# Layer-norm statistics moved from VectorE to ScalarE, with new slacks, a new opening and a new end, in a kernel of two FFNs around a selective scan

## The reference

```python
x = x + 0.5 * ffn(layernorm(x))
x = x + mamba(layernorm(x))
x = x + 0.5 * ffn(layernorm(x))

def ffn(x):    # 512 -> 1408 -> 512, ternary weights with a scale per row
    return ((silu((x @ gate_w.T) * gate_s) * ((x @ up_w.T) * up_s)) @ down_w.T) * down_s

def mamba(x):  # I = 1024 channels, N = 16 states, R = 128
    h, gate = split(x @ W_in.T)
    u = silu(causal_conv4(h) + conv_b)
    ts, B, C = split(u @ Wx.T);  ts, B, C = rms(ts), rms(B), rms(C)
    delta = softplus(ts @ Wdt.T + dt_bias)
    # per channel i, state n:  s = exp(delta * A[i, n]) * s + delta * u * B[n];  y += s * C[n]
    return ((y + D * u) * silu(gate)) @ Wout.T
```

## Time and profile before

| what | value |
|---|---|
| median of three runs | 3033.19 us |
| profiled execution, its own time | 3031.56 us |
| span from first to last instruction | 3029.6 us |
| busy: PE / DVE / POOL / ACT | 81% / 82% / 75% / 58% of the span |
| mean granted TensorE clock | 0.888 of full speed |
| first scan instruction | 207.15 us |
| x of the last chunk stored to `out` (issue) | 3022.30 us |

### The profile page before, as it was taken

The page is one execution under the profiler, slowest core; times in us unless marked ns, Lnnn a source line. Parts: engine busy times, 40 slices in busy tenths (PEclk is TensorE's granted clock), DMA queues, the critical chain, the costliest instruction groups (busy, mean ns, idle before and its releaser), DMA issues. The chain is left out here.

```text
span 3029.6 us, 37464 instructions
## 1 busy us (share of the span) xinstructions
PE 2454.4 (81%) x12266; PEld 1988.6 (66%) x12266; DVE 2487.0 (82%) x3129; ACT 1769.5 (58%) x3005; POOL 2262.2 (75%) x1372
## 2 busy tenths in 40 slices
PE   7567776967787799778998899888997796697878
PEld 5456555756666677667776677666775675576666
DVE  5539897879988889599977899799987988899952
ACT  5456566565765667465566667665566566654522
POOL 2237767886997778777888679978898778997832
PEclk9778797978798899898998899999998897798899
DMA  7543562664286645884478555974478555556464
GB/s 278 193 160 130 185 221 67 199 228 163 89 277 235 224 138 179 309 275 157 136 255 298 206 167 172 321 280 144 156 245 291 187 165 187 202 181 242 136 219 136
DMA packets 294953, 608.70 MB, mean 201 GB/s; under 512 B 23008, under 2 KB 23776, under 8 KB 294752
## 3 DMA queue, kind: packets, MB, share of 16 engines
q1 hardware_dynamic: 294752, 606.23, 59.6%
HBM read 453.57 MB, written 152.57 MB: 200 GB/s over the span
## 5 line engine op out<-in xcount | busy, mean ns | idle before, releaser
L1104 POOL TENSOR_TENSOR sbuf<-dus,bring 128x1024 f32<-128x1024 f32 x512 | 1219.1, 2395 | 314.6 <-PE pt L1144 229.2
L512 PE MATMUL pm<-xT,wring 128*128 128x512 f32 x4352 | 1132.5, 409 | 89.2 <-DVE xT L535 30.4
L512 PEld LDWEIGHTS pm<-xT,wring 128*128 128x128 f32 x4352 | 821.5, 195 | 262.9 <-issue 83.8
L1118 ACT ACTIVATE pa<-dls,cst 128x512 f32<-128x512 f32 x1024 | 692.0, 688 | 482.5 <-DVE sbuf L1127 439.6
L1144 PE MATMUL pt<-ident,sbuf 128*128 128x128 f32 x4096 | 678.3, 306 | 263.4 <-DVE sbuf L1127 154.2
L1144 PEld LDWEIGHTS pt<-ident,sbuf 128*128 128x128 f32 x4096 | 532.1, 157 | 424.4 <-DVE sbuf L1127 204.5
L1127 DVE TENSOR_TENSOR_SCAN sbuf<-pa,carry,sbuf 128x512 f32<-128x512 f32 x512 | 635.7, 1269 | 72.7 <-POOL sbuf L1104 38.1
L1127 DVE TENSOR_TENSOR_SCAN sbuf<-pa,sbuf 128x512 f32<-128x512 f32 x512 | 605.4, 1209 | 83.0 <-ACT pa L1118 46.8
L584 PE MATMUL pm<-wring,act 128*128 128x512 f32 x2176 | 588.7, 416 | 58.9 <-DVE hd L1040 28.2
L1155 DVE SCALAR_TENSOR_TENSOR acc<-pt,cT,acc 128x512 f32<-128x512 f32 x768 | 549.1, 741 | 95.9 <-PE pt L1144 87.9
L584 PEld LDWEIGHTS pm<-wring,act 128*128 128x128 f32 x2176 | 410.5, 197 | 157.5 <-DVE hd L1040 33.4
(11 more groups left out here) (133 smaller groups left out, 2086.9 us busy)
## 6 DMA issues: line engine op xcount, KB each, us to landing
wring<-wsp SPq DMA_DIRECT2D x408, 512.0 KB, 4.3
bring<-b_d SPq DMA_DIRECT2D x256, 256.0 KB, 3.8
xn_d<-tb SPq DMA_DIRECT2D x24, 1024.0 KB, 9.0
xnb<-xn_d SPq DMA_DIRECT2D x21, 1024.0 KB, 7.4
x_d<-tb SPq DMA_DIRECT2D x16, 1024.0 KB, 5.7
u_d<-hd SPq DMA_DIRECT2D x64, 256.0 KB, 3.8
sg_d<-hd SPq DMA_DIRECT2D x64, 256.0 KB, 4.0
tb<-x_d SPq DMA_DIRECT2D x16, 1024.0 KB, 7.1
```

The source lines that it names most:

```text
L512: f = lambda e, pw=pw, px=px, k=k, first=(i == 1), end=(i == total): e.matmul(pm[b][:, 0:n], lhs(pw, k), rhs(px, k), start=first, stop=end)
L1104: t_p = S.op("pool", lambda e, s2=s2, s3=s3, h=h: e.tensor_tensor(sbuf[:, s3, h * m:(h + 1) * m, :], dus[:, h * m:(h + 1) * m, :], bring[: ...
L1118: t_e = S.op("act", lambda e, k=k, i=i, pb=pb, n=n: e.activation(pa[pb][:, :], dls[:, k, :], ACT.Exp, scale=col(C_A + i * N + n)), dl_tok[ ...
```

## The change

`STATS = "act"`: except for three norms (chunk input 0, chunk 0 after FFN 1, the last chunk after the scan) ScalarE takes the statistics: a pass with a row sum per tile, POOL makes -mean of it, and a second pass squares the differences and sums them. Both passes write their elementwise result to `tb[:, 0:4]`, which must be free for it. The other edits: thread T gets a slack of 0.3 on VectorE and 0.5 on PE; `prep_in` of chunks 1 and 2 too is fed straight from `tb` (DIRECT); chunk 0's convolution works in PSUM with three tiles open and its projection steps behind the loop; parts 0 and 1 of chunk 0's softplus go into thread L, without the 12 us, and their u is loaded into `dus` beforehand; `dus` is freed and loaded by halves; in the last `post` blocks 4 to 7 are made inside the projection, in the banks `pt` and `pa`; in the last `tail` two of four additions go to VectorE and each tile is stored by itself.

```diff
-SLACK_T = 0.0
+SLACK_T = 0.3
+SLACK_S = 0.0
+SLACK_TP = 0.5
+STATS = "act"
+DIRECT = (0, 1, 2)
+DEPTH0 = 3
+SOFT0 = True
+LASTPOST = True
+LASTOUT = True
-WITH_CONV = (0,)
+WITH_CONV = ()
-... "t": dict(pe=0, dve=3, act=3, pool=3, slack_dve=SLACK_T), "s": dict(act=4, dve=4, pool=4)}
+... "t": dict(pe=0, dve=3, act=3, pool=3, slack_dve=SLACK_T, slack_pe=SLACK_TP), "s": dict(act=4, dve=4, pool=4, slack_dve=SLACK_S)}
...
+        def stats(tt, t_x, free, quick=True):
+            if quick:
+                t = L.op("dve", lambda e: e.bn_stats(st[:, tt, :], tb[:, 4 + tt, :]), t_x)
+                return L.op("dve", lambda e: e.bn_aggr(mv[:, tt, :], st[:, tt, :]), t, *free.get("mv", ()), n=16)
+            return L.op("act", lambda e: e.activation(
+                tb[:, tt, :], tb[:, 4 + tt, :], ACT.Copy, accum_out=mv[:, tt, 0:1]), t_x,
+                *free.get("mv", ()), *free.get("tb0", ()), more=0.25)
+        def normalise(free, ln_out, s, c, t_mv, quick=True):
+            m = 1.0 if quick else 1.0 / H
+            t = L.op("pool", lambda e: e.tensor_scalar(nb[:, :], mv[:, :, 0], -m, 0.0, ALU.mult, ALU.add), t_mv, ...
+            if not quick:
+                for tt in range(4):
+                    t_mv = L.op("act", lambda e, tt=tt: e.activation(
+                        tb[:, tt, :], tb[:, 4 + tt, :], ACT.Square, bias=nb[:, tt:tt + 1],
+                        accum_out=mv[:, tt, 1:2]), t, more=0.25)
+            t = L.op("pool", lambda e: e.tensor_scalar(ve[:, :], mv[:, :, 1], m, EPS, ALU.mult, ALU.add), t_mv, n=16)
...
+            quick = STATS == "dve" or c == 0                                  # pre_norm
+                quick = STATS == "dve" or (s, c) in ((1, 0), (2, NCH - 1))    # tail
+                at_end = LASTOUT and last_out and c == NCH - 1
                 for k in range(nk):
+                    if middle and k == 4:
+                        middle()
...
-                        t_r = M.op("pool", lambda e, tt=tt: e.tensor_tensor(
+                        t_r = M.op("dve" if at_end and tt % 2 else "pool", lambda e, tt=tt: e.tensor_tensor(
                             tb[:, 4 + tt, :], tb[:, tt, :], tb[:, 4 + tt, :], ALU.add), t_o, t_x)
+                        if at_end:
+                            t_s = M.dma(st_x, x_dst[c * TC + tt * P:c * TC + (tt + 1) * P, :], tb[:, 4 + tt, :], t_r)
...
-                t_xT = ready_xT((1, c)) if c else make_xT(first_xn[-1], tb)
+                t_xT = make_xT(first_xn[c], tb) if c in DIRECT else ready_xT((1, c))
...
-                    if opened:
-                        finish()
                     opened.append((i, r, b, t_c))
-                    if c not in TWO_OPEN:
+                    while len(opened) >= (1 if c else DEPTH0):
                         finish()
...
+                ahead = SOFT0 and (c, part) in ((0, 0), (0, 1))
+                X = L if ahead else D
+                stay = c == 0 and part < 2
+                if stay:
+                    t_u = D.dma(l_du[i0], dus[:, i0:i0 + 2, :], u_d[c, i0:i0 + 2].rearrange("k p n -> p k n"),
+                                u_tok[i0], u_tok[i0 + 1], t_small[0])
...
-                t_l = D.op("act", lambda e: e.activation(e_, e_, ACT.Ln, bias=1.0), t_q,
-                           n=n, table="ln")
+                t_l = X.op("act", lambda e: e.activation(e_, e_, ACT.Ln, bias=1.0), t_q,
+                           n=n, table="ln0" if ahead else "ln")
...
+                def second_half():            # post, chunk 7: passed to tail as middle
+                    for i in range(4, NI):
+                        block(i)              # turned in pt and pa instead of pm
...
-                                          *sf("du"))
+                                          *sf(("du", k // 2)))
...
+                        if n == N - 1:
+                            sfree["du", h] = (t_p,)
+                            if ig == 0:
+                                for k in range(h * m, (h + 1) * m):
+                                    load_u(1, k)
...
-            INPLACE = ("prep_in", 0), ("ffn2", NCH - 1)
+            INPLACE = *(("prep_in", c) for c in DIRECT), ("ffn2", NCH - 1)
```

More of the change, by code:

```diff
@@ L560, in build, with tail @@
             last_xn = []
-            first_xn = list(begun.get("first_xn", []))
+            first_xn = dict(begun.get("first_xn", {}))
             free.update(begun.get("free", first_free))
-            def tail(nk, first_piece, scale, t_act, x_src, x_dst, s, c, last_out=False):
+            def tail(nk, first_piece, scale, t_act, x_src, x_dst, s, c, last_out=False, middle=None):
                 if first:
@@ L606, in tail @@
                     if not last_out:
-                        t_mv = stats(tt, t_r, free)
+                        t_mv = stats(tt, t_r, free, quick)
+                if at_end:
+                    stores.append(t_s)
+                    return
                 if scale is None:
@@ L616, in tail @@
                 else:
-                    t_xn = normalise(free, ln_out, s, c, t_mv)
-                    if s == 1 and c == 0:
-                        first_xn.append(t_xn)
+                    t_xn = normalise(free, ln_out, s, c, t_mv, quick)
+                    if s == 1 and c in DIRECT:
+                        first_xn[c] = t_xn
                     if s == 2 and c == NCH - 1:
@@ L707, in prep_in @@
                 even = c % 2 == 0
-                t_xT = ready_xT((1, c)) if c else make_xT(first_xn[-1], tb)
+                t_xT = make_xT(first_xn[c], tb) if c in DIRECT else ready_xT((1, c))
                 if c + 1 < NCH:
                     pre_norm(free, ln_out, c + 1)
-                if c == 0 and c not in WITH_CONV:
+                if c in DIRECT and c not in WITH_CONV:
                     prefetch(0)
@@ L820, in prep_in @@
                         x_step(i - XLAG)
-                if opened:
+                while opened:
                     finish()
@@ L988, in softplus_steps @@
                 yield True
-                t_l = D.op("dve" if c == 0 else "pool", lambda e: e.tensor_tensor(e_, e_, w_, ALU.subtract),
+                t_l = X.op("dve" if c == 0 else "pool", lambda e: e.tensor_tensor(e_, e_, w_, ALU.subtract),
                            t_l, n=n)
-                t_u = D.dma(l_ud, w_, u_d[c, i0:i0 + 2].rearrange("k p n -> p k n"),
-                            u_tok[i0], u_tok[i0 + 1], t_l)
-                stay = c == 0 and part < 2
+                if not stay:
+                    t_u = D.dma(l_ud, w_, u_d[c, i0:i0 + 2].rearrange("k p n -> p k n"),
+                                u_tok[i0], u_tok[i0 + 1], t_l)
@@ L1027, in post, with block @@
                 y_src = [ysb[:, 0], acc if c == NCH - 1 else ysb[:, 1]]
-                for i in range(NI):
+                split_end = LASTPOST and c == NCH - 1
+                def block(i):
                     r, q, v = i % 3, i % 5, i % 5
@@ L1046, in post @@
                     a_tok.append((t_hi, t_lo))
-                free["xT"] = (t,)
-                for q in range(2):
-                    free["th", q] = u_free[q]
-                for q in range(2):
-                    free["aa", q] = g_free[q]
+                    if i == NI - 1:
+                        free["xT"] = (t,)
+                        for q in range(2):
+                            free["th", q] = u_free[q]
+                            free["aa", q] = g_free[q]
+                for i in range(4 if split_end else NI):
+                    block(i)
+                def second_half():
+                    for i in range(4, NI):
+                        block(i)
                 next_xT("post")
-                tail(NI, WO, 0.5, a_tok, x2_d, x3_d, 2, c)
+                tail(NI, WO, 0.5, a_tok, x2_d, x3_d, 2, c, middle=second_half if split_end else None)
             y_ready = {}
```

71 lines of the change are left out of this document (34 added, 37 removed).

## The result

The changed kernel takes 3013.9 us in the median of 12 runs against 3030.4 for the kernel before: ratio 0.995, 95% interval 0.9934 to 0.9966. It is faster, by 15 us (10 to 20) and not by 72. The profiled execution took 3009.1 us, span 3007.3.

A forecast was written before the change was run, and what follows sets the result against it. No engine was full, VectorE nearest (87% from 220 to 2905 us), beside two streams ending together. Terms -25 - 24 - 7 - 5 - 4 - 7 = -72 gave 2960 us; range 2905 to 3030, some 0.82.

The forecast's parts named there:

- the statistics' term: Stretch from 220 to 2905 us: moving the norms' statistics to ScalarE gives -24 us (bounds -54 to +40).
- The first rival: Chain of layers, PE and its hand-overs, decides; VectorE's relief does not shorten M's matmuls: -35, 2997 us; chance 0.20.
- Its price: ScalarE's two statistics passes: 1.53 us a tile over 80 tiles, 122 us more work on ScalarE.
- the 14 foretold: Scan's exponentials queued behind ScalarE's statistics: 0.35 us for each of 40 bursts, 14 us, at most 40.
- The slower rival: ScalarE's in-order queue holds up the scan, at 6 us a norm: +82 for the statistics, 3065 us; chance 0.12.
- sign of a wait for `pa` above 150 us: Scan's wait for ScalarE's exponential: at most 100 us expected; above 150 the slower rival is at work.
- The opening: Start of the kernel: chunk 0's convolution -13 and first softplus -12, together -25 us (-36 to 0).
- the slacks: Planned accumulations on VectorE and transposes on PE put off, aimed at VectorE's 87.9 us wait: -5 us, uncertain by 25.
- direct chunks: Chunks 1 and 2 fed straight from `tb`, without the trip through DRAM: -7 us (-20 to 0).
- halves: Loading `dus` by halves starts one POOL product 2.4 us earlier in up to 13 waits: -4 us (-15 to 0).
- End: Last projection and last tail: -2 and -5, together -7 us; slower quarter stores could make it -3.
- wrong altogether: Sign at the scan's end: a last accumulation after 2900 us would show the forecast wrong.

The follow-up runs named there:

- four orders: Planner's matmul factor at 1.11, 1.12, 1.13 and 1.14, for either kind of statistics with all other edits: mean ratio 0.9826 with VectorE's, 0.9946 with ScalarE's.
- this factor: The planner's matmul factor (`PEF`) of 1.12, against the kernel before: ratio 0.9783 with VectorE's statistics, 0.995 with ScalarE's.

## Why the prediction was wrong

The step that failed is the statistics' term: "Of the 54 us I credit 70%, since 13% of the stretch is VectorE idle which its relief does not shorten: -38 + 14 = -24". The runs put +51 in its place, above its upper bound of +40 (+37 in the mean of four orders, +5 in the kernel before without the other edits). That the changed kernel still lies between 2905 and 3030 is luck: this term missed by 75 us one way, the other edits together by 18 the other way.

- *Its credit.* VectorE's busy time fell by 45 us, and no run shows a gain from it: taking 33 us off VectorE by short statistics, at the order of the kernel with VectorE's statistics, gained nothing. A share of 87% was read as the bound. The first rival, that the chain of layers decides, came nearer: the part of the loss that was found sits in that chain. But its -8 for the statistics had the wrong sign too.
- *Its price.* A tile took 0.62 + 0.71 = 1.33 us of ScalarE, less than the 1.53 estimated, and ScalarE gained 97 us instead of 122. At the order kept, shortening both to some 0.59 us (0.25 and 0.34 over 64 columns) weighed 7 us.
- *What is queued behind.* "Queued behind them are the scan's exponentials" named the wrong victim. Their wait is 5 us longer than with VectorE's statistics at this factor, 17 in the mean of the four, so the 14 foretold were about right and are not the loss. What was pushed back at chunk 2's edge was softplus, which lived in the very gap that ScalarE has there while it waits for VectorE. That the longer norm "shows only where nothing lies between it and its reader" is the same miss: at chunk 2's edge the norm took as long as with VectorE's statistics (13.0 us against 12.9), and its neighbours came later.
- *The slower rival* had the right queue and the wrong passenger. Its sign of a wait for `pa` above 150 us did not come, yet the move did cost, some 2.4 us for each of the 21 norms if the 51 us are spread evenly. The Trainium skill, "ScalarE: Activation LUTs", Rules for kernel authors, gives addition and multiplication to VectorE; the runs bear the advice out for these norms (37 us in the mean of four orders), though less by the price of the passes than by what stood behind them: the same shortening was worth 7 us in one order and 41 in another.
- *Other edits.* Forecast -48, measured -66 at this order and -53 in the mean of the four. The opening brought 16.5 us at its second product, not 25: u came within 3 us of the time foretold, but the x-projection behind it ran 11 us longer. The convolution thus handed on some 5 us early (softplus's last input is ready at 181.6 instead of 186.3), not 13; the first scan instruction gained 3. The waits that the slacks aim at fell by 24 us on VectorE and 60 on POOL, but POOL's fell as far in the kernel before with the move alone (161.5 us), which has no slacks; VectorE's did not (87.2). POOL's wait for `dus`, which the halves aim at, rose from 43 to 55 us. Between the traces of the kernel before and of the one with VectorE's statistics, 39 of 60 us lie between the first statistics of chunk 1's and chunk 3's FFN 1 tails (546.6 and 507.6 us), where chunks 1 and 2 are fed straight from `tb`; the forecast had 7 us for that edit. No run undoes slacks, direct chunks or halves by themselves, so their shares are not shown.
- *End.* From the scan's last accumulation to the end 123.6 us, within the 120 to 124 foretold: 5.2 us less than before, where the sum had 7; the 3 that were estimated for slower quarters did not come. The scan's last accumulation ends at 2883.7, 17 us earlier than before, so the sign for "wrong altogether", one after 2900, did not show. For a sum of 72 us that threshold was too loose.
- *The forecast's accuracy.* Four orders of the changed work lie between 2979 and 3039, so a spread of nearly half the prediction's range comes from the planner's order, which no row of before shows.

## What to carry to other kernels

Before work moves to an engine with room, look at what that engine does while it waits for the result that it would now make itself: if another chain lives in that gap, the move takes its place, however low the busy share is. In a kernel with an order written out by a planner, measure a change at three or four neighbouring planner settings before judging it: here one setting shows a cost of 5 us and another 51.

## What the hardware showed besides

A row sum or square with an accumulator holds ScalarE for its whole pass: four sums stand 0.61 us apart, as `L333` at 638.32, 638.93 and 639.54 in the changed kernel, though each is followed by an accumulator read of 0.19 us. Passes without an accumulator overlap by 0.09 us: the four of `L351`, 0.80 us each, take 2.92 us together, so they stand 0.71 apart.

An instruction of VectorE on 512 columns with both operands in SBUF took 0.69 us while POOL was idle (`L422` at 185.48), 1.27 beside POOL's addition (`L625` at 2998.25), and 2.8 beside POOL's products (three of `L422` in 8.38 us from 195.64).
